# A decoder layer with its attention steps issued in another order, and without the idle matmuls of the last batch

## What is computed

```python
x = x + attn(layernorm(x))             # causal self attention, 16 heads of 16
x = x + xattn(layernorm(x), ctx_1024)  # cross attention to 77 context rows
x = x + ffn(layernorm(x))              # quantized: silu(gate) * up, then down
```

## Time and profile before

| | us |
|---|---|
| median of three runs | 989.03 |
| the profiled execution, first to last instruction | 989.7 |
| before the first `pv` of the second half of the first head group (head) | 0 to about 92 |
| attention of all batches (body) | to 797.9 |
| what is left of batch 3 after its self attention scores (tail) | 797.9 to about 891 |
| feed-forward layer | about 891 to 989.7 |

### The profile page before, as it was taken

The page is one execution under the profiler, slowest core; times in us unless marked ns, Lnnn a source line. Parts: engine busy times, 40 slices in busy tenths (PEclk is TensorE's granted clock), DMA queues, the critical chain, the costliest instruction groups (busy, mean ns, idle before and its releaser), DMA issues. The chain is left out here.

```text
span 989.7 us, 17256 instructions
## 1 busy us (share of the span) xinstructions
PE 906.5 (92%) x6014; PEld 442.7 (45%) x6014; DVE 708.9 (72%) x1466; ACT 602.1 (61%) x1121; POOL 312.7 (32%) x348
## 2 busy tenths in 40 slices
PE   4788899999999989999999999999999989989976
PEld 2424343446444624364435433554343554543344
DVE  3788875767866792877767747678675548687987
ACT  2233477764667577646677566366688734647975
POOL 1242216420331216521422056223421123303633
PEclk9877999999999999999999999999999999998999
DMA  5240111334222151111221304112210162114009
GB/s 163 93 130 8 52 54 59 75 79 49 89 73 86 36 167 51 62 33 36 95 85 31 128 25 116 49 33 76 91 64 3 43 189 87 46 43 159 13 1 191
DMA packets 83568, 73.42 MB, mean 74 GB/s; under 512 B 19244, under 2 KB 79788, under 8 KB 83484
## 3 DMA queue, kind: packets, MB, share of 16 engines
q1 hardware_dynamic: 78540, 68.58, 22.8%
q0 software_dynamic: 4256, 3.21, 2.5%
q10 hardware_dynamic: 688, 0.53, 0.2%
HBM read 19.81 MB, written 13.13 MB: 33 GB/s over the span
## 5 line engine op out<-in xcount | busy, mean ns | idle before, releaser
L777 ACT ACTIVATE probs<-psum 128x512 f32<-128x512 f32 (+1 forms) x608 | 314.7, 577 | 184.9 <-PE psum L972 181.7
L1144 DVE CUSTOM_DVE_ANT_0 junk<-psum,mask 128x640 bf16<-128x640 f32 (+3 forms) x256 | 253.4, 1022 | 62.8 <-PE psum L936 61.1
L698 POOL TENSOR_SCALAR_AFFINE_SELECT probs<-probs 128x512 f32<-128x512 f32 x128 | 81.3, 637 | 396.2 <-ACT probs L777 395.9
L972 PE MATMUL psum<-q_stack,k_stack 98*128 98x512 bf16 (+3 forms) x768 | 189.3, 332 | 7.5 <-DMA q_stack<-max_rows 3.4
L997 PE MATMUL psum<-probs,v_sb 128*17 128x512 f32 (+3 forms) x1536 | 160.2, 496 | 3.8 <-POOL probs L698 3.4
L1140 DVE TENSOR_REDUCE rowmax<-psum 128x4 f32<-128x512 f32 (+2 forms) x96 | 97.6, 1045 | 64.5 <-PE psum L930 64.1
L936 PE MATMUL psum<-k_stack,q_stack 96*128 96x512 bf16 (+3 forms) x512 | 129.0, 345 | 7.0 <-DVE rowmax L1144 4.7
L972 PEld LDWEIGHTS psum<-q_stack,k_stack 98*128 98x128 bf16 x768 | 63.1, 98 | 137.5 <-ACT probs L777 80.6
L896 PE MATMUL psum<-xnT,wT 128*128 128x512 f32 x192 | 91.4, 607 | 0.6 <-ACT xnT L742 0.3
L821 PE MATMUL psum<-wT,xnT 128*128 128x256 f32 x384 | 87.2, 384 | 0.5 <-ACT xnT L742 0.3
L821 PEld LDWEIGHTS psum<-wT,xnT 128*128 128x128 f32 x384 | 73.1, 193 | 12.5 <-ACT xnT L742 1.4
(11 more groups left out here) (182 smaller groups left out, 1246.8 us busy)
## 6 DMA issues: line engine op xcount, KB each, us to landing
q_stack<-q_parts SPq DMA_DIRECT2D x192, 64.0 KB, 2.6
k_stack<-k_parts SPq DMA_DIRECT2D x192, 64.0 KB, 2.6
xq_stack<-xq_parts SPq DMA_DIRECT2D x168, 64.0 KB, 2.6
xn<-in_x SPq DMA_DIRECT2D x8, 512.0 KB, 4.9
res<-in_x SPq DMA_DIRECT2D x4, 1024.0 KB, 6.9
out<-res SPq DMA_DIRECT2D x8, 512.0 KB, 2.9
normT_hbm<-xnT SPq DMA_DIRECT2D x6, 512.0 KB, 3.5
xf<-normT_hbm SPq DMA_DIRECT2D x6, 512.0 KB, 3.6
```

The costliest lines, as they stand in the source:

```text
L698: nc.gpsimd.affine_select(out=tile, in_=tile, compare_op=ALU.is_ge, fill=0.0, base=0, pattern=[[0, GH], [1, P]], channel_multiplier=-1).th ...
L777: nc.scalar.activation(probs[n % 2][:, heads * k:heads * k + heads, 0:cols], bank_a(s)[:, 0:heads * cols].rearrange("p (h n) -> p h n", h= ...
L972: last = nc.tensor.matmul(bank[:, cols * n:cols * n + cols], k_stack[:, slot, h, P * j:P * j + P], q_stack[:, slot, half, h, q0 - HALF * h ...
L1144: nc.vector.tensor_tensor_reduce(out=junk[D_STEPS.place(s) % 2][:, 0:keys], in0=bank_d(s)[:, 0:keys], in1=m.mask[:, T - keys:T], scale=1.0 ...
```

## The change

All letters of `PICKS` stay, in another sequence; most steps move by fewer than 20 places, some by up to 343. `fillers` and its loop go. VectorE waits before each `xmax` for the one before it. Cut to its core:

```diff
 PICKS = (
-    "pppppppkppppppkkvppqqkkmpmmpppmmmpmmppppqqmmmmmmqqsssmssmmsrsqqmmsvmssmvsmmvvvmmpmmvssmmssmssmssmqvmssmv"
+    "ppppppppppkkkkpppkvppqqmmpppmmpmmpmmppppkqqqqkmmmmmmsmsssmsmsmvmsssmsmmvsmmvvvkkmmpmvmsssmssmssmsmqqvmss"
 ...
-    "scvvvvxxrwxxxxxyyyyyxxxyyxwwwwwwyyyycccwwcccccccccdcdddcwdcccddcddccddccdcdddccccddddcddccwwccddddcddccw"
-    "ddcddccdxxdyxccwwddddxxddxwdxdddddwddxdyyxwwxxxwyyyyyywwwyyy")
+    "vxxwxxxrxxxxycxxyyyyyxxyxxwwyyyycccccwwcwccdcwcdcccddxwcwwcccdddcddccdddccdcddccwccdddcdddccccdddcdddccc"
+    "cddddcwddxxccwwwdddxxdxxxddddddydddxddyywwwwwyyyyyyyxxxwwwyy")
 ...
-def fillers(s):
-    ...
-        return 2 if kind == "xy" else 1 if kind == "xs1" and s[3] % 2 == 0 else 0
-    return 0
 ...
             for s in ORDER:
-
-                for _ in range(fillers(s)):
-                    nc.tensor.matmul(psum[:, 7, :], m.identb[:], m.mask[:, 0:HALF], start=True, stop=True)
 ...
                 if s[0] == "xmax":
 ...
+                    if XMAXES.place(s):
+                        dve.wait_ge(xmax_done, XMAXES.place(s))
```

More of the change, by code:

```diff
@@ L324 @@
-    "mmsssmmdvvvxmssdsssccdcddvmssdvssqqmsddmcdddmvsvsccmmssdvsmsvddddmvdmmssdmddccsscsccddcssmdvscmmsssvscms"
-    "sddddmsvssmmssdvssdmmddvsddvvvssdsvssdsssvssxvsxxxvvvsssxsssxxxxxssxxxvssssvsssvssssxxsvssxxxsvsxrxxssvx"
-    "scvvvvxxrwxxxxxyyyyyxxxyyxwwwwwwyyyycccwwcccccccccdcdddcwdcccddcddccddccdcdddccccddddcddccwwccddddcddccw"
-    "ddcddccdxxdyxccwwddddxxddxwdxdddddwddxdyyxwwxxxwyyyyyywwwyyy")
+    "ppppppppppkkkkpppkvppqqmmpppmmpmmpmmppppkqqqqkmmmmmmsmsssmsmsmvmsssmsmmvsmmvvvkkmmpmvmsssmssmssmsmqqvmss"
@@ new lines @@
+    "smsmvmmvmssmsmssmssmsmvmsssmksmvmssmvsvmqqmmmvvmvqqssmssmssmsspvssvspmmvsssmmsvvssmsmvqsspsmmvssmmssspvk"
+    "ssmmsssvsmmqsssvssmmppppvmmsmmpmvvvmssqqmssvsssmsvssvsmmpmmvvvsssmqmpspssmmvsssmmssvssmmsssvsssmmsvssmqs"
+    "msvssvmmsmmpmvvvmssmssvssmssvrssqqmvsmmvsqmssmvvsssmmvmssmssmvssmmsssvssmmssqsvsskkmssmvssvmmmspmmvvvsss"
+    "mvssskkvssvmqqvvsmmsspmmpmmvvkvrssmmcxxxsmmxssxxxxmsssxvsssvssmqmsssxvsssvsxssxmmssvsqxxvssqmmxqxxxcmmmm"
+    "mxmmvvvmmsmssmssvssscvmsscvscccvsssvcccmsmssvsmxcmddvsddqccmxmmsddcdcssvccddcccssdvsmssmssdcdddcdmscqsdv"
@@ new lines @@
+    "ccsdmdmddsvdmccsccsssddddvdcmscdvccddmddmmdsmdddmddqmqssmddmdmddvvxmmdmssdsvssmxxmxmxxxxxxvsxsmvsvssvvss"
+    "sxxmssvsssxxxxmmsxxxxxsvssvsmsssmssmvsssmxmpppsppvssvsvsssvssssspppppvpppvpvvsspsppppvvvqqmmsssmsmssmssm"
+    "vsssqqmmvmqssmssmsqmvmsmsssmmvssmmssvsmmsvscqmvmvvpmmmvvvssmxxmssmsqsmssmvsmsmvmmvmssmxmsrrssmvxmxvxxsss"
+    "xvssmmxxsssvssssmvsmsssvsssmxxxsvssqmmvsxxxxvmmxqmmxmmsvvmsssvsmsssqqmcvmssmvmscvscssmsvsccvscssvccsmmcs"
+    "sxscccqdvddccdxccmddmmdddvsssmmsdmsssdddmddmcsvcssmssccddccdddvccccsqsdvmmcdddmddmsccqdcdddvvccdvmmdvddd"
@@ new lines @@
+    "dmdmssdqmdmdddmsmssmdsmsdsmvxmxssmmxxxmxxxxxxxxvvsssxsxxxsvvsssvssssvxxxxxxmssmssvmsssmssmvssvmmssssvspp"
+    "pppvsspvpvssspvssppppppsvspsqqppvspppqqmmvmqssmssmvvmsvmssmmssmssmsmvmmvmssmssmssmssmvsmsssmvmssqvsmmmmm"
+    "vvvmmsssvssvvrssmsvsqqmsmvmsmvssmmssvvsmssmvsssmmsvmsxmssmvmsssmxmxxrxxxsssvssqmxxmqmssvssxxxxmvsvsssmsv"
+    "xxxxcxmmsssvmsqqxmvvssmmvscmmvssmsmsvsvcssccsvscssqcsvssccmmssvsscmmssxdcmvssscmsddmcxmmdvqdvmmsscsmddmd"
+    "dcvvvxdccccsmsqqssdssvsscvssmddmdmdvvssmccssscdvmmvsssvdcccmsdcddmvsssmmdssmmsvccssscsdddcddvcsscmmssdmd"
@@ L329 @@
+    "dmddmvdmssdddmddsvmmssddddvdssvvdssvssdssvssxvsxxxvvvsssxxsssxxxsxsvsssvssxsssxxvsssvsssssvssvsxxrxxvvvx"
+    "vxxwxxxrxxxxycxxyyyyyxxyxxwwyyyycccccwwcwccdcwcdcccddxwcwwcccdddcddccdddccdcddccwccdddcdddccccdddcdddccc"
+    "cddddcwddxxccwwwdddxxdxxxddddddydddxddyywwwwwyyyyyyyxxxwwwyy")
 ORDER = order_of(PICKS)
```

## The result

The kernel after is slower: 1000.75 us median of four runs against 987.56 of four runs of the kernel before, ratio 1.0134 (95% interval 1.0101 to 1.0167). I had forecast 984.0 with a range of 973 to 994. Its profiled execution spans 999.9 us, before 989.7.

A forecast was written before the change was run, and what follows sets the result against it. Head and tail were priced apart from a body with PE nearly always busy; the tail is a serial chain through all engines. Terms -12 - 2 + 7 + 2.5 + 1.5 - 2 = -5 gave 984.0 us, range 973 to 994.

The forecast's parts named there:

- My terms: Head and body -14; late store with low clock behind it +9.5; tail without idle matmuls +1.5; tail's gains -2 us.
- The head: Head: earlier q and splits, bias moved away, less half clock; -12 us, from -7 to -16.
- so I see nothing that takes it back before the body: Head: its gain is kept up to the body, since DVE, PE and SP all move together.
- the -2 that I gave the body: Body: steps move by a few places, no gap surely closes for nothing; -2 us, from -8 to +4.
- rival B: Head: gain only -6 instead of -12, as PE idles elsewhere and low clock returns; 990 us, chance 13%.
- The bias: Head: moving POOL's 4.52 us addition away from DVE's rstd chain wins 2.6 us, plus 1.5 of half clock.
- The store: Tail: tstore.2.1, issued behind the weight loads, lands late and delays ACT's copy; +7 us, bounds +2.7 and +8.0.
- Half clock behind it: Tail: after PE's wait for the store, o starts at 1.2 GHz; +2.5 us, from 1.7 to 3.4.
- Rival A: Tail: store not late, its packets pass between the weights' or the ring has drained; 977 us, chance 25%.
- The clock: Tail: without idle matmuls, first cross scores and last norm mostly wait, with small PE work; +1.5 us, from 0 to 5.
- rival C: Tail: PE at 1.2 GHz for 25 us of real chain work; another 9 to 10 us, 994 us, chance 12%.
- What the tail wins: Tail: fewer stalls from last stack on, about -5, less costs of split, bias and xmax; -2 us, from -4 to +1.

The follow-up runs named there:

- run 1: New order up to place 1720, then the old order with its idle matmuls, against the kernel before: 982.69 us, ratio 0.9923.
- run 3: Kernel after with the weight loads moved from ahead of the last store of the transposed batch to behind it: 990.82 us, ratio 1.0029 to before.
- run 5: Kernel after with the second tstore ahead of the weight loads and the idle matmuls back: 989.18 us, ratio 0.9971 to before.
- run 8: New order to place 1720, old behind, idle matmuls kept, cstore.1 and cstore.2 moved behind the stack.5 DMAs: 973.85 us, ratio 0.9825 to before.
- run 13: Kernel after with store ahead of weights, idle matmuls back, xs2.3.0.0 behind xs1.3.2, cstore.1 and cstore.2 behind stack.5: 979.83 us, ratio 0.9904 to before.
- run 11: Kernel before with bias.0.0 moved behind s1.1.0.9, where POOL was idle: 985.27 us, ratio 0.9964.
- run 9: Kernel before with only the first 40 steps of the new list, old order behind: 983.05 us, ratio 0.9945.
- run 10: Kernel before with bias.0.0 moved from place 104 to behind cstore.1, among maxima read from PSUM: 991.08 us, ratio 1.0006.
- Run 6: Kernel before with wload moved ahead of tstore.2.1 on the SP queue: 999.03 us, ratio 1.0086.
- run 14: run 8 with rload.3, the 1 MB residual load, moved from ahead of tstore.2.1 to right behind it: 973.23 us, ratio 0.9843 to before.
- run 2: Kernel before without its 102 idle matmuls, nothing else changed: 997.01 us, ratio 1.0068.
- run 12: run 5 with xs2.3.0.0 moved behind xs1.3.2 in the tail, as in the old list: 990.2 us, ratio 1.0000 to before.

## Why the prediction was wrong

By ratios, the difference of +13.3 us falls into: head and body -7.6 (run 1), the store +10.4 (run 3), the idle matmuls +5.7 (run 3 to run 5), the rest of the tail's order +4.7 (run 5 to run 1). By the intervals each of these is good to 4 to 6 us. My terms were -14, +9.5 with the half clock behind it, +1.5 and -2. Against them the head and body came out 6.4 us dearer, the store 0.9, the idle matmuls 4.2 and the tail's order 6.7.

- **The head, right; the body, where the first step failed.** `s1.0.0.6` starts at 47.9 (I had 47), the first `pv` of the second half at 75.0 (77 to 80), and no operation of DVE takes 4.9 us there. That is 15.7 us of lead, at the upper end of my 7 to 16. The step that failed is "so I see nothing that takes it back before the body", and the -2 that I gave the body: the body takes it back. `cstore.1` and `cstore.2` stand ahead of `stack.5.q.1` in the new list, 10 us of issue on SP, and of the 15.7 us 8.6 are left at place 492. With them behind the stacks the lead there is 16.4 us (run 8), and the time falls by 9.5 to 9.7 us (runs 8 and 13). The size is near rival B's (6 instead of 12), but not its cause alone: an in-order queue made the wait, and the low clock only followed it. No gap of the kernel before contains it; the order of SP's queue in the new list does, and I didn't read that past the head. From place 492 to 1745 the new list wins another 1.4 us.
- **The bias, right in its mechanism.** Run 11 keeps 3.6 us by its ratio (interval 1.4 to 5.6); I had 2.6 for the stall and 1.5 for the half clock behind it, 4.1. The Trainium skill, "SBUF — State Buffer", section "SBUF: two separate sides", says that DVE and GpSimd share a pair of ports as an exclusive lock, which the first to start holds for its whole instruction; a DVE operation with two SBUF inputs needs it against a GpSimd operation that reads SBUF. The traces agree that the operation of the `rstd` chain, which has two such inputs, lasts until the addition of 4.5 us ends (4.92 and 4.97 us instead of 0.17). They differ from the page in who holds the ports: by the records DVE's operation starts 0.36 and 0.42 us ahead of the addition (76.47 against 76.83, 67.72 against 68.14 in run 9) and is the one held up. Reductions from PSUM beside the same addition aren't held up, 1.22 us each in run 10.
- **The store, right.** ACT's idle time before the copy is 10.21 us, 7.0 more than before. The copy starts 21.7 us behind place 1745 instead of 14.0, 7.6 more; I had 7, from 2.7 to 8.0. Half clock behind it I had at 2.5; run 3 gives 10.4 for both. Run 6 shows the same cost in the old list. Rival A (packets pass between those of the weights) falls: the store lands 1.3 us after the last weight load. The Trainium skill, "DMA: Bandwidth & Descriptors", section "Queues, rings and completion order", says that the write that signals completion lands only after every earlier write of the same DMA engine. By it the store can't be seen as landed before those writes of the weights that went ahead of it on its engines, and the trace agrees. What I had wrong is the 3.20 us of before: I called the store the end of that wait, and run 14 shows that a second chain ended with it. It didn't matter for the sum, because the new wait is compared with the same copy.
- **The clock, mis-sized.** I gave the idle matmuls 1.5 us, 0 to 5. They are worth 4.6 to 5.7 in the new list and 6.7 (3.4 to 10.1) in the old. I had written that the densest part of the tail has little waiting and so would stay at full clock. That was read from a trace in which idle matmuls filled the waits: 102 of them, 22 us. Without them PE is busy for 27.5 of 32 us from 829 and the granted clock is 0.52, both during and after a stretch with waits of 2.61 and 2.52 us. That is rival C, which I had given 12%. Its condition, 17 us of path work at half clock, was met if most of those 27.5 us lie on the path, which no run here measures; its price, 9 to 10 us on top of the 1.5, was too high: the removal cost 10.1 in all at the upper end of run 2's interval.
- **What the tail wins, wrong in sign.** I had -2, from -4 to +1; it is +4.7 by runs 5 and 1, and 6.0 to 7.8 by run 13 against runs 14 and 8. The weights' pieces, which I moved out of one wait in my working, stand in another now (run 12); which other places cost the rest stays open. The two `xmax` at the very end are no part of the miss: I had 1.5 us for them, and they start 1.64 us apart:

```profile
897.31 1.22 DVE L1166 TENSOR_REDUCE bmax<-xn 128x1 f32<-128x1024 f32 x1
...
898.95 1.22 DVE L1166 TENSOR_REDUCE bmax<-xn 128x1 f32<-128x1024 f32 x1
```

Three misses had the same sign, so a sum of -5 became +13. To hold 1000.75 the range would have needed a small gain of head and body, C, and a tail order that costs time, all together.

## What to carry to other kernels

When a static order is changed, read every in-order queue from end to end for what now stands ahead of a transfer that someone waits for: both large losses here (10 us each) are DMAs that nobody needs yet, issued ahead of one that PE or ACT needs at once, and with two steps moved, the new head and body in front of the old tail are 1.7% faster than the old list. A granted clock of 0.99 in a stretch with idle matmuls says nothing of the clock without them; the bound for their removal is half clock over all the work of the stretch, not over its waits alone. It is a bound and no price: 31.06 us of work at 0.50 would be 15.5 us longer than at full clock, an estimate from run 2's row, and the run lost 6.7. And before a wait is called a cost, ask what would end it if its releaser came early: here it was another engine, at the same moment.

## What I had not expected of the hardware

Half clock outlasts the waits that it follows by far more than in the head, where a stretch of 3.4 us stood in the earlier trace rows: with the idle matmuls out, PE is busy for 31.06 of 37.00 us (old list) and for 27.50 of 32.00 (new list) and stays at 0.50 to 0.52 all that time. At half clock `xy` takes 1.94 us instead of 1.06.

Nor do the same instructions in the same order always get the same clock. The old tail with its idle matmuls takes 94.5 us in the trace of before and 94.6 in run 1's, but 99.2 in run 8's and 99.1 in run 11's. PE alone for 14 us, from about the 40th us of the tail on, before and run 8:

```profile
837.00:851.00 14.00, 12.88 (x119) 1.00 0.31 99
```

```profile
818.00:832.00 14.00, 11.93 (x70) 0.63 0.31 102
```

PE's longest wait in or just ahead of the second stretch is 0.80 us. What makes the difference no run here shows; it is a part of the spread of single runs, and the reason for pricing changes of 0.5% by many runs and not by one trace.

SP's own issue can be the slow part: in the trace of the kernel after, the `xv_hbm<-xprobs` DMAs of `cstore` took from 0.85 to 5.81 us each to issue when several stood in a row, and the queue behind them moved by that much.
